# AdaLN block on one core: fp16 pairs for the normed rows, wa, w1, w2 and hid, gelu left in PSUM, output product in three products, new instruction orders

## The reference

```python
sa, ca, ga, sb, cb, gb = (silu(c) @ wmod) in six parts     # one row per batch
h  = layernorm(x) * (1 + ca) + sa
# attention block on h, 16 heads of 16, causal window of 128
a  = layernorm(h) * ln1_w + ln1_b
q, k, v = a @ Wq + bq, a @ Wk + bk, a @ Wv + bv
h  = h + softmax(q k' / 4 + band) v @ Wo + bo
h  = h + gelu(layernorm(h) @ W1 + b1) @ W2 + b2            # 256 -> 1024 -> 256
x  = x + ga * h
# second half
h  = layernorm(x) * (1 + cb) + sb
xr, xk = mu * h + (1 - mu) * (h one row earlier)            # two mixes
x  = x + gb * sigmoid(xr @ W_r) * (square(relu(xk @ W_k)) @ W_v)
```

## Time and profile before

| | before |
|---|---|
| median of 3 runs | 693.57 us (692.31 to 695.18) |
| the profiled execution's own time | 697.08 us |
| its span, first to last instruction | 695.4 us |
| TensorE busy | 617.6 us (89%) |
| VectorE busy | 534.7 us (77%) |
| ScalarE busy | 469.9 us (68%) |
| GpSimd busy | 384.4 us (55%) |
| mean granted TensorE clock | 0.983 of full |

### The profile page before, as it was taken

The page is one execution under the profiler, slowest core; times in us unless marked ns, Lnnn a source line. Parts: engine busy times, 40 slices in busy tenths (PEclk is TensorE's granted clock), DMA queues, the critical chain, the costliest instruction groups (busy, mean ns, idle before and its releaser), DMA issues.

```text
span 695.4 us, 18126 instructions
## 1 busy us (share of the span) xinstructions
PE 617.6 (89%) x6798; PEld 538.1 (77%) x6798; DVE 534.7 (77%) x1113; ACT 469.9 (68%) x810; POOL 384.4 (55%) x516
## 2 busy tenths in 40 slices
PE   6976979899789999898989899898999999899986
PEld 4655868888677878788877878796878788889975
DVE  5568685577697889888988899789978888756653
ACT  2425555658597878787778777977877786864432
POOL 5102426654648483857666665756584738765430
PEclk9999898999999999999999999999999999999999
DMA  3452321243023131232122313321221222001110
GB/s 122 147 149 54 85 63 56 69 119 84 19 54 109 43 75 38 80 87 75 39 72 87 85 39 86 86 71 46 66 69 52 66 56 77 32 6 43 32 38 31
DMA packets 56868, 47.06 MB, mean 68 GB/s; under 512 B 26235, under 2 KB 48061, under 8 KB 56782
## 3 DMA queue, kind: packets, MB, share of 16 engines
q1 hardware_dynamic: 53798, 43.85, 22.6%
q10 hardware_dynamic: 2984, 2.05, 1.2%
HBM read 18.11 MB, written 4.23 MB: 32 GB/s over the span
## 4 chain that ended last, share of the span: by engine, by line
PE 45%; issue 15%; ACT 13%; POOL 12%; DVE 12%; ACTq 1%; DMA 1%; DVEq 0%; POOLq 0%; SPq 0%
ACT p L862 5%; PE bank L225 4%; DVE nmax L1290 3%; PE bank L403 3%; PE bank L345 3%; PE bank L446 3%; PE bank L420 3%; PE bank L458 2%; PE bank L422 2%; PE bank L421 2%; PE quad L321 2%; PE bank L405 2%; PE bank L404 2%; POOL p_lo L1866 2%; PE quad L288 2%
## 5 line engine op out<-in xcount | busy, mean ns | idle before, releaser
L862 ACT ACTIVATE p<-quad,scale_s 128x384 f32<-128x384 f32 (+1 forms) x256 | 120.6, 541 | 35.4 <-PE quad L321 30.8
L1853 POOL TENSOR_SCALAR_AFFINE_SELECT p<-p 128x448 f32<-128x448 f32 x64 | 45.6, 712 | 119.6 <-ACT p L862 119.6
L1866 POOL TENSOR_TENSOR p_lo<-p,p_hi 128x1344 f16<-128x1344 f32 x32 | 89.6, 2800 | 20.3 <-ACT p_hi L872 20.2
L872 ACT ACTIVATE p_hi<-p 128x1344 f16<-128x1344 f32 x64 | 84.8, 1327 | 14.1 <-POOL p L1858 12.3
L1290 DVE TENSOR_REDUCE nmax<-quad 128x8 f32<-128x1032 f32 x64 | 78.9, 1234 | 2.2
L403 PE MATMUL bank<-bt_hi,w_hi 128*128 128x256 f32 x256 | 76.5, 299 | 0.8 <-ACT hid L926 0.8
L420 PE MATMUL bank<-w_hi,hid_hi 128*128 128x256 f32 x256 | 75.2, 294 | 0.2 <-DVE hid_lo L1372 0.2
L321 PE MATMUL quad<-q_st,k_st 100*128 100x192 f16 (+2 forms) x512 | 60.8, 242 | 15.3 <-DVE qt_lo L1265 6.7
L405 PE MATMUL bank<-bt_hi,w_lo 128*128 128x256 f32 x256 | 72.3, 283 | 0.0
L404 PE MATMUL bank<-bt_lo,w_hi 128*128 128x256 f32 x256 | 72.3, 282 | 0.0
L422 PE MATMUL bank<-w_hi,hid_lo 128*128 128x256 f32 x256 | 72.3, 282 | 0.0
(11 more groups left out here) (201 smaller groups left out, 1787.3 us busy)
## 6 DMA issues: line engine op xcount, KB each, us to landing
k_st<-kt_hi SPq DMA_DIRECT2D x120, 64.0 KB, 2.0
v_blk<-vn SPq DMA_DIRECT2D x64, 66.0 KB, 2.2
x<-x SPq DMA_DIRECT2D x16, 256.0 KB, 2.8
out<-x SPq DMA_DIRECT2D x16, 256.0 KB, 2.2
q_st<-qt_hi SPq DMA_DIRECT2D x120, 32.0 KB, 1.9
k_st<-kt_lo SPq DMA_DIRECT2D x60, 64.0 KB, 2.0
xa<-x SPq DMA_DIRECT2D x7, 512.0 KB, 4.4
hid<-w_ff SPq DMA_DIRECT2D x2, 1024.0 KB, 6.4
```

Source lines behind the costliest of these rows:

```text
L862: e.activation(p32[gp % 2][:, i * 2 * QW:i * 2 * QW + w], ring_s.at["st", gp, i][:, 0:w], ACT.Exp, scale=scale_s[:, 1:2]).then_inc(s_ex, 1)
L1866: e.tensor_tensor(cut(p_lo), p32[gp % 2][:, :].rearrange("p (n c) -> p n c", c=QW), cut(p_hi), ALU.subtract).then_inc(s_plp, 1)
```

## The change

- `wa`, `w1`, `w2`, `at`, `bt` and `hid` keep their two parts in fp16 instead of fp32r. So that the numbers stay in fp16's range, the chip sums squares of w1, w2 and the bias of the first product at the start (`setup_sq1`, `setup_sq2`, `setup_f1`, `setup_f2`, `setup_s1`, `setup_s2`), and scales by the inverse roots; the scales are taken back in gelu's input scale, and in `add_y`.
- `gelu` writes its result over its input in PSUM. `high_f` moves from VectorE to ScalarE and reads PSUM; `low_f` reads PSUM instead of SBUF. A bank of `up` is released by `low_f` (`s_hl`) instead of the second gelu.
- `out_project` was one fp32 product; it is three fp32r products of `ct_hi`, `ct_lo` and `wo_hi`, `wo_lo`. VectorE gets a new stage `low_c` per turn, and a bank of `transposes_c` is released by it.
- `hid` as a staging place is gone: w1 and w2 have their own tiles, and the load of w2 is the second thing SyncE issues, ahead of the load of w_attn.
- All five orders are written anew. At the start the four `maxima` of turn 0 follow each other directly, with `setup_mod_rest` and both `values` behind them; in the loop the four `up` have other work between them. `warm` has 161 calls instead of 188.

```diff
-        wa_hi, wa_lo = sb("wa_hi", [P, KC, 3 * D], F32R), sb("wa_lo", [P, KC, 3 * D], F32R)
+        wa_hi, wa_lo = sb("wa_hi", [P, KC, 3 * D], F16), sb("wa_lo", [P, KC, 3 * D], F16)
...
-                        last = e.matmul(dst, ct[:, k, ts], wo[:, k, :], start=(k == 0), stop=(k == KC - 1))
+                        e.matmul(dst, ct_hi[:, k, ts], wo_hi[:, k, :], start=(k == 0), stop=False)
+                        e.matmul(dst, ct_hi[:, k, ts], wo_lo[:, k, :], start=False, stop=False)
+                        last = e.matmul(dst, ct_lo[:, k, ts], wo_hi[:, k, :], start=False, stop=(k == KC - 1))
...
-                    bank, free = ring_b.take(("f1", i, m2), s_gl, 8 * i + 2 * m2 + 2)
+                    bank, free = ring_b.take(("f1", i, m2), s_hl, 4 * i + m2 + 1)
...
-                    e.activation(hid[:, m, :], ring_b.at["f1", i, m // 2][:, (m % 2) * 2 * P:(m % 2 + 1) * 2 * P],
-                                 ACT.Gelu_apprx_tanh, bias=bias_1[:, m:m + 1]).then_inc(s_gl, 1)
+                    dst = ring_b.at["f1", i, m // 2][:, (m % 2) * 2 * P:(m % 2 + 1) * 2 * P]
+                    e.activation(dst, dst, ACT.Gelu_apprx_tanh, bias=bias_1[:, m:m + 1], scale=scale_g[:, 0:1]).then_inc(s_gl, 1)
+
+            def high_f(i, first, last_):
...
+                for m in range(first, last_):
+                    e.wait_ge(s_gl, 8 * i + 2 * m + 2)
+                    e.activation(hid_hi[:, 2 * m:2 * m + 2, :], ring_b.at["f1", i, m][:, :].rearrange("p (m n) -> p m n", m=2), ACT.Copy,
+                                 scale=inv_f[:, 1:2]).then_inc(s_hh, 1)
...
-                    e.tensor_tensor(hid_lo[:, 2 * m:2 * m + 2, :], hid[:, 2 * m:2 * m + 2, :], hid_hi[:, 2 * m:2 * m + 2, :].bitcast(F32),
-                                    ALU.subtract).then_inc(s_hl, 1)
+                    e.scalar_tensor_tensor(out=hid_lo[:, 2 * m:2 * m + 2, :], in0=ring_b.at["f1", i, m][:, :].rearrange("p (m n) -> p m n", m=2),
+                                           scalar=inv_f[:, 1:2], in1=hid_hi[:, 2 * m:2 * m + 2, :], op0=ALU.mult,
+                                           op1=ALU.subtract).then_inc(s_hl, 1)
...
+            def low_c(u):
...
+                e.tensor_tensor(ct_lo[:, u % 2, :], ring_s.at["ctr", u][:, :], ct_hi[:, u % 2, :].bitcast(F32), ALU.subtract).then_inc(s_cl, 1)
```

More of the change, by code:

```diff
@@ L351, in transposes_c @@
                     return
-                bank, free = ring_s.take(("ctr", u), s_ct, u + 1)
+                bank, free = ring_s.take(("ctr", u), s_cl, u + 1)
                 e.wait_ge(s_cx, 4 * (u + 1))
@@ L572, in _ @@
-            maxima(1, 0)
-            warm(13, 4)
-            maxima(1, 1)
-            warm(14, 2)
-            maxima(1, 2)
-            warm(15, 5)
-            transposes_a(1)
-            warm(16, 2)
+            maxima(1, 0)
+            maxima(1, 1)
+            warm(7, 6)
+            maxima(1, 2)
+            warm(8, 10)
+            scores(1, 2, 4)
+            transposes_a(1)
+            context(0)
+            warm(9, 3)
+            maxima(1, 3)
+            warm(10, 3)
+            project(2)
@@ L580, in _ @@
+            warm(11, 3)
             scores(2, 0, 2)
+            context(1)
+            warm(12, 3)
             scores(2, 2, 4)
[L582 to L594 removed]
+            scores(3, 0, 2)
+            max_rows(1)
@@ L595, in _ @@
+            warm(13, 1)
+            scores(3, 2, 4)
+            warm(14, 6)
+            maxima(2, 0)
+            warm(15, 4)
+            setup_mod_rest()
+            warm(16, 1)
+            scores(4, 0, 2)
+            warm(17, 5)
+            scores(4, 2, 4)
+            warm(18, 1)
             maxima(2, 1)
-            warm(22, 2)
             context(2)
-            scores(4, 0, 2)
-            warm(23, 1)
-            scores(4, 2, 4)
+            warm(19, 12)
+            scores(5, 0, 2)
@@ L627, in _ @@
-            context(6)
-            scores(9, 2, 4)
-            warm(30, 2)
-            maxima(3, 0)
-            warm(31, 2)
+            maxima(3, 0)
+            context(6)
+            warm(25, 1)
+            scores(8, 0, 2)
+            warm(26, 1)
+            scores(8, 2, 4)
+            warm(27, 3)
+            scores(9, 0, 2)
+            scores(9, 2, 4)
+            warm(28, 1)
             context(7)
-            warm(32, 1)
             scores(10, 0, 2)
-            warm(33, 6)
+            warm(29, 4)
@@ L679, in _ @@
             context(11)
-            warm(51, 8)
+            scores(14, 0, 2)
             values(2, 0)
-            scores(14, 0, 2)
+            transposes_c(2)
+            warm(44, 7)
             down(0, 0)
-            scores(14, 2, 4)
-            transposes_c(2)
-            scores(15, 0, 2)
-            down(0, 1)
-            maxima(4, 2)
-            context(12)
             for b in range(2, B):
                 u, gp = 2 * b, 8 * b
-                keys(u - 5)
+                receptance(u - 5)
+                scores(gp - 2, 2, 4)
+                context(gp - 4)
+                maxima(u, 2)
+                down(u - 4, 1)
+                scores(gp - 1, 0, 2)
@@ L1654, in _ @@
+            normalise(9)
+            stats_x(3)
+            low_b(0)
+            low_qk(4)
+            low_p(11)
+            maxima(4, 0)
+            low_f(0, 0, 1)
+            normalise(10)
+            low_f(0, 1, 2)
+            setup_w2()
             residual_a(1)
-            low_p(11)
-            high_f(0, 1, 2)
-            high_f(0, 2, 3)
+            stats_b(1)
             maxima(4, 1)
-            low_f(0, 1, 2)
+            low_f(0, 2, 3)
             normalise(11)
-            high_f(0, 3, 4)
@@ new lines, in _ @@
+                low_qk(u + 2)
+                low_p(gp + 1)
+                gated(u - 4)
+                residual_b(u - 3)
+                low_p(gp + 2)
+                low_p(gp + 3)
+                low_f(u - 2, 0, 1)
+                low_f(u - 2, 1, 2)
+                maxima(u + 2, 0)
+                normalise(gp + 2)
+                low_f(u - 2, 2, 3)
+                residual_a(u - 1)
+                output(u - 4)
+                normalise(gp + 3)
+                low_f(u - 2, 3, 4)
@@ L1967, in _ @@
             select(2)
+            setup_f1()
             select(3)
```

939 lines of the change are left out of this document (482 added, 457 removed).

## The result

The changed kernel takes 699.41 us (median of 19 runs, 695.0 to 704.71), the kernel before 695.18 in the runs beside it: a ratio of 1.0054, 95% interval 1.0028 to 1.0081. It is slower by half a per cent, and the forecast of 672 us and its range up to 693 us were wrong. The profiled execution is one of the shorter ones, 696.02 us, with a span of 694.3 us against 695.4 before: what the median has lost beside that is in no profile here. Of the 19 runs, those under 697.1 us have a mean granted clock of 0.970 to 0.975, those over 701 us 0.956 to 0.966; whether the clock makes them long or follows from TensorE's waits is not shown.

The account below looks back on a forecast made before the run. TensorE was taken to lead, idle for only 6.15 us of a 73.1 us loop period, its waits ended by exps. End -3, six periods -15.6 and start -3 gave -21.6 us: 693.6 to 672 us, range 650 to 693.

Parts of the forecast that it names:

- No engine alone asks for more than 64 us: Loop period: TensorE's work falls to 62.6 us, ScalarE's rises to 63.2, VectorE's is 61.6.
- 60% of TensorE's saving: Loop: only this part of TensorE's 4.4 us comes out, -2.6 us a period, from 73.1 to 70.5.
- The fp16 step: TensorE: a 256-column product takes 0.108 us in fp16 instead of 0.120 in fp32r, 2.3 us a period for 192.
- The extra at a group's first product: TensorE: 0.08 us more for a group's first product goes with fp32r weights; 0.8 us a period, bounds 0 and 1.6.
- not 0.62 us: ScalarE: each `high_f` copy out of PSUM was priced at 0.62 us, eight a period, +5.0 us.
- my bound (0.55): ScalarE: gelu keeps 0.470 us; writing PSUM bounded by 0.40 and 0.55 us, -1.1 to +1.3 us a period.
- VectorE's 61.6: VectorE's busy time a period, from 63.65: `high_f` lost 3.5 us, `low_c` added 1.4, `low_f` unchanged.
- The start: Before the loop: first scores 3 us earlier (9 earlier to 4 later), w_attn late by 0 to 6 us.
- The end: Last three half-batches: -3 us (-6 to +3), from cheaper products, against banks held longer.
- the second: Rival: exps and maxima over the four banks hold the loop at 73.1 us; 688 to 691 us; chance 0.17.
- The banks of `up`: Rival: TensorE waits for banks held longer, up to 1.5 us each; 697 or 706 us with four or five exposed; chance 0.17.
- the sign that I had given for it: Waits profile: `hid_lo` named ahead of `up` or `transposes_d` with several us a period would mean the banks decide.

Follow-up runs that it names:

- experiment 8: Kernel before with fp16 parts alone, plus `high_f` moved from VectorE to ScalarE behind each second gelu: 717.75 us, 1.0293 of the kernel before.
- experiment 4: Kernel before with the parts of wa, w1, w2, at, bt and hid in fp16 and nothing else, no scales: 686.53 us, 0.9859.
- experiment 1: Changed kernel with SyncE's loop order alone altered, next batch's input and stacks issued ahead of the second store: 690.15 us, 0.9911 of the kernel before.
- 7: Experiment 1's kernel with only the scales of gelu and w1 left out: 681.98 us, 0.9804 of the kernel before.
- 6: Experiment 1's kernel with scales left out of gelu, `high_f`, `low_f`, w1, w2 and `add_y`: 677.85 us, 0.9728 of the kernel before.
- 5: Experiment 1's kernel with `high_f` also shortened to 64 of 512 columns from the second half-batch on: 678.64 us, 0.9742 of the kernel before.
- experiment 12: Experiment 1's order without scales, with w1, w2, bt and hid back in fp32r, projections in fp16: 691.47 us, 0.9938 of the kernel before.
- experiment 2: Changed kernel with gelu written to SBUF, `high_f` and `low_f` reading it there, banks of `up` freed by the second gelu: 707.44 us, 1.0164.
- 3: Changed kernel with `high_f` doing 32 of each 256 columns from the second half-batch on: 686.67 us, 0.9861 of the kernel before.
- 9: Experiment 4's kernel with the output product in three products and `low_c` on VectorE ahead of the maxima: 708.48 us, 1.0161 of the kernel before.

## Why the prediction was wrong

**The step that failed** is "No engine alone asks for more than 64 us", and the period of 70.5 us drawn from it with 60% of TensorE's saving. It foresaw a gain of 2.6 us in a period and there was a loss of 0.8 (73.9 against 73.2, means of four). It had ScalarE's load at 63.2 us, as measured, and gave it no price. The runs price it: ScalarE's work sits in one queue with the exps, which the quad ring waits for, so it comes out for a half or more. 4.5 us more in a period cost 4.8 to 5.2 (experiment 8 against 4, in the old order and with the banks of `up` left alone); the gelu's scale operand, 1.4 us, cost 1.3 (1 against 7); all the scale operands, 2.1 us of ScalarE by their groups (16 x 0.088 + 8 x 0.09) and 0.5 of VectorE, cost 1.55 (1 against 6); but 2.6 us of `high_f` cost only 1.35 (1 against 5). Experiments 5, 6 and 7 all end at 70.5 to 70.8 us, with 60.6, 61.5 and 61.9 us of ScalarE; what holds the period there was not tried. TensorE's saving, against it, was worth 37% in the old order (1.25 us of period for 3.4 of busy time, experiment 4) and 61% in the new (1.4 for 2.3, experiment 12). I weighed the two by busy share, where the waits in the earlier trace rows already named exps. So the mechanism was wrong in what it left out, a price for ScalarE, and the 60% was too much for the old order.

**The queue that had no step.** My working went through SyncE's order at the start only. In the loop the kernel before too has a store ahead of the next stacks, but its wait there is 9.4 us. The change puts `load_residual`, `load_x` and `load_mod_g` in between as well, and in its new order the store's data come later: 24.7 us of wait, with a SyncE that takes each in turn. Experiment 1 prices that at 1.43 points, 10 us: more than the whole slowdown of 0.54. In the loop it is 1.85 us of a period, by the profiles.

**The terms.** The fp16 step is right (0.108 against 0.1096 us), and `low_c` took 0.686 us as foreseen. The extra at a group's first product went as foreseen, from 0.20 to 0.12 us (`up`, 301.95 to 302.07 us in the changed kernel), but TensorE's busy time fell by 3.4 us in a period with fp16 alone and by 3.1 in the change, not by 4.4. `high_f` took 0.690, not 0.62 us: the earlier trace rows had the answer, for of the two copies out of PSUM I quoted, the one with a vector operand (`qt_hi`, bias) took 0.687 and the one without (`bt_hi`) 0.587. The gelu took 0.533 us, inside my bound (0.55) for a reason that I hadn't named: the bound was for the PSUM write, but that lowers it (0.445 with the same operands as before's 0.470), and the new scale operand raises it by 0.088. The Trainium skill ("ScalarE: Activation LUTs", "What ACT_TABLE_LOAD costs") says that each per-partition operand adds about 93 ns to an ACTIVATE; the runs agree with 88 and 90. The same page of the Trainium skill also says ("Step-by-step: what each stage is for") that PSUM is the quicker destination for ScalarE, and the runs agree, with 25 ns and, at experiment 2, 20. VectorE's `low_f` went from 0.706 to 0.748, 6% over what I had kept, and is 0.685 without its scale operand. By their single times `high_f` and the gelu took 1.6 us a period more than my terms for them, so that 63.2 came out for ScalarE has luck in it. VectorE's 61.6 was 60.1: `mix` no longer stands beside GpSimd's `low_p` and takes 3.3 us less, and no term of mine had that.

**The start** was too small. The load of w2 ahead of `w_attn` delayed nothing visible, the first product of `project` stands at 26.48 us (27.08 in the earlier trace rows). The first scores come at 47.8 us instead of 55.4, 7.6 us earlier, and 6.2 of it are left at 218 us, though the granted clock is 0.88 over the first 143 us instead of 0.94. What that clock costs was not tried: it is 0.86 to 0.89 in every kernel of the new order looked at (1, 2, 3, 5, 6, 7, 12). **The end** was wrong in sign: it takes 2.1 us more instead of 3 less. With fp16 alone it gains 4.4; without the scales it is 4.3 shorter than in experiment 1, and with the short `high_f` (3 and 5) as much. So there too ScalarE's new work has eaten the products' saving.

**The rivals.** The nearest of them was the second (gain stays in the quad ring, with "a ScalarE with 5 us more work in front of those exps"): its mechanism is what experiment 8 shows, but it was priced as a gain lost, at 688 to 691 us, and not as a loss; and its sign, more than 3.0 us of the maxima's waits for exps, did not come (1.8 us). The banks of `up` were the rival with the right sign and, by the sign that I had given for it (`hid_lo` ahead of `up`, 1.6 us and 2.5 for the weight loads), it seemed confirmed. But the fastest kernel still has 1.1 and 1.6 us of these waits in a period of 70.5 us, experiment 1 leaves them as they are (1.6 and 2.4 us) and gains 10 us, and taking them away gave no gain. That they cost nothing isn't shown, since experiment 2 changed other durations too.

**The sum of it**, in points of the kernel before: fp16 -1.41; the rest +1.95, of which SyncE's order is 1.43 and the scale operands 1.83 (experiment 1 against 6). These two make more than the rest, so without them the other parts (new order, output product, gelu in PSUM, `high_f` on ScalarE, earlier start) together gain 1.3, to which the earlier start (6.2 us) and perhaps the quicker `mix` belong. How those 1.3 divide wasn't tried: they can't be put one by one into the old order at the places tried without the losses of experiments 8 and 9, and the gelu kept in PSUM wasn't tried in the old order at all.

## What to carry to other kernels

Price an instruction by the queue that it goes into, not by its engine's busy share: on the engine whose results end the waits, 4.5 us more were 4.8 us of time in one place and 2.6 us less were 1.35 in another, while the busiest engine's savings were worth 37 to 61% of a period. Where a change reorders a program, read each DMA queue of it for what now stands behind a wait; a wait for a store's data ahead of the next batch's transfers cost more here (1.43 points) than the change's slowdown (0.54). And count vector operands: a scale taken from memory instead of a constant costs 0.09 us an instruction, which on 192 small activations was 17 us of ScalarE.

## What the runs showed of the hardware

- The type that an engine writes didn't matter: `high_f` 0.600 us and `low_f` 0.685 us with fp16 results, 0.600 and 0.686 with fp32r (experiments 6 and 12).
- VectorE's scalar operand costs too: `low_f` 0.748 us with the scale from memory, 0.685 with a constant, 0.06 us each.
- A two-input operation on VectorE took as long from SBUF as from PSUM (median 0.750 us both, experiment 2 and the changed kernel), while its copy took longer from PSUM (0.681) than from SBUF (0.436).
- A VectorE operation with two inputs in SBUF took twice as long and more beside certain GpSimd operations on SBUF: `mix` 4.50 us for four beside `low_p`, 1.66 without (kernels before and after); `low_f` up to 1.76 us instead of 0.75 (experiment 2). A mean over a group hides this; look at its median and longest.
- Each stack DMA occupies SyncE's queue for about 0.6 us, so that 24 of them are 17 us from the first to the last (312.27 to 329.06 us).
- In experiments 2, 8 and 9 the granted clock was 0.98 over the period instead of 1.00. TensorE's idle time in the whole period doesn't tell it: the changed kernel's second period has 11.0 us of it at 1.00, experiment 2's 10.4 us at 0.98.
